# A macaron block in one kernel: hand-written orders for the opening and for the last four bodies

## What is computed

```python
x = L0_attn_x                                   # (2, 4096, 512)
x = x + 0.5 * _L0_ffn_ref(_layernorm(x), ...)   # first half
x = x + _L0_attn_ref(_layernorm(x), ...)        # causal linear attention, 16 heads of 32
x = x + 0.5 * _L0_ffn_ref(_layernorm(x), ...)   # second half

# at the end of _L0_ffn_ref
y = t + outs
yn = (y - mu) * jax.lax.rsqrt(var + 1e-05) * ln_g + ln_b

# attention, per head: phi(u) = elu(u) + 1
S = S + pk_t[..., :, None] * v_t[..., None, :]  # running state over the 4096 positions
z = z + pk_t
num = jnp.einsum('bhd,bhde->bhe', pq_t, S)
den = jnp.sum(pq_t * z, axis=-1, keepdims=True) + EPS
out = (num / den) @ Wo.T + bo
```

## Time and profile before

| | us |
|---|---|
| Time before, median of 3 runs | 940.27 (939.8 to 940.8) |
| Time of the profiled execution | 940.58 |
| Span of the profiled execution, first to last instruction | 938.8 |
| PE matmul busy | 898.5 (96%) |
| DVE busy | 827.4 (88%) |
| ACT busy | 758.4 (81%) |
| POOL busy | 711.6 (76%) |

### The profile page before, as it was taken

The page is one execution under the profiler, slowest core; times in us unless marked ns, Lnnn a source line. Parts: engine busy times, 40 slices in busy tenths (PEclk is TensorE's granted clock), DMA queues, the critical chain, the costliest instruction groups (busy, mean ns, idle before and its releaser), DMA issues. The chain is left out here.

```text
span 938.8 us, 29969 instructions
## 1 busy us (share of the span) xinstructions
PE 898.5 (96%) x10252; PEld 525.8 (56%) x10252; DVE 827.4 (88%) x1531; ACT 758.4 (81%) x1327; POOL 711.6 (76%) x875
## 2 busy tenths in 40 slices
PE   3899999999999999999999999999999999999974
PEld 2455556555555655555565555556565555655542
DVE  6888899999999999999999999999999999998764
ACT  5978788888888888888888888888888888888861
POOL 2277787788777788878778987777898777779761
PEclk9999999999999999999999999999999999999986
DMA  8286887866687666768767666876766787776762
GB/s 290 41 174 123 171 159 156 138 153 151 144 179 156 149 142 148 151 148 179 156 146 144 146 151 151 179 156 141 146 149 148 154 171 161 144 121 128 128 118 68
DMA packets 421405, 139.81 MB, mean 149 GB/s; under 512 B 402544, under 2 KB 402544, under 8 KB 421360
## 3 DMA queue, kind: packets, MB, share of 16 engines
q1 hardware_dynamic: 404496, 106.73, 60.5%
q10 hardware_dynamic: 16864, 32.51, 10.6%
HBM read 21.76 MB, written 16.78 MB: 41 GB/s over the span
## 5 line engine op out<-in xcount | busy, mean ns | idle before, releaser
L1302 PE MATMUL PJ<-wT,XT 128*128 128x512 f16 x2304 | 525.1, 379 | 1.7 <-DMA XT<-XH 1.4
L1302 PEld LDWEIGHTS PJ<-wT,XT 128*128 128x128 f16 x2304 | 216.6, 98 | 245.3 <-DMA XT<-XH 3.2
L459 POOL TENSOR_TENSOR A<-AM,A 128x512 f16<-128x512 f32 x256 | 292.5, 1162 | 35.4 <-ACT A L677 35.4
L1401 PE MATMUL PJ<-wT,AT 128*128 128x512 f16 x768 | 178.6, 383 | 1.2 <-DMA AT<-ATTN 1.2
L451 POOL TENSOR_SCALAR_AFFINE_SELECT AM<-AM 128x512 f32<-128x512 f32 x128 | 82.0, 641 | 113.1 <-ACT AM L667 113.1
L677 ACT ACTIVATE A<-AM 128x512 f16<-128x512 f32 x256 | 154.0, 630 | 12.6 <-POOL AM L451 11.3
L1372 PE MATMUL AV<-SS,QS 128*128 128x33 f16 x1024 | 112.3, 178 | 4.9 <-POOL A L459 4.4
L1375 PE MATMUL AV<-VN,A 128*128 128x33 f16 x3072 | 116.9, 178 | 0.0
L1401 PEld LDWEIGHTS PJ<-wT,AT 128*128 128x128 f16 x768 | 71.6, 98 | 79.8 <-issue 2.7
L1375 PEld LDWEIGHTS AV<-VN,A 128*128 128x128 f16 x3072 | 109.3, 96 | 3.7
L992 DVE TENSOR_TENSOR AM<-SC,causal 128x512 f32<-128x512 f32 x128 | 87.5, 684 | 22.9 <-PE SC L1352 22.9
(11 more groups left out here) (101 smaller groups left out, 1531.8 us busy)
## 6 DMA issues: line engine op xcount, KB each, us to landing
out_dram<-Y ACTq DMA_DIRECT2D x32, 512.0 KB, 3.1
X<-in_L_attn_x_dram ACTq DMA_DIRECT2D x30, 512.0 KB, 3.5
X<-in_L_attn_x_dram SPq DMA_DIRECT2D x2, 512.0 KB, 8.0
A<-in_L_attn_Wk_dram SPq DMA_DIRECT2D x1, 1024.0 KB, 8.3
A<-in_L_attn_Wq_dram SPq DMA_DIRECT2D x1, 1024.0 KB, 10.5
QS<-in_L_attn_Wv_dram SPq DMA_DIRECT2D x1, 1024.0 KB, 12.7
QS<-in_L_attn_Wo_dram SPq DMA_DIRECT2D x1, 1024.0 KB, 16.0
XT<-XH SPq DMA_TRANSPOSE x64, 3.4
```

The lines of the kernel that those rows point to most:

```text
L459: g.tensor_tensor(A[:, b, LO, hg], AM[:, k % 4], A[:, b, HI, hg], ALU.subtract).then_inc(a_lo.sem, 1)
L1302: ins = t_.matmul(PJ[b], XT[:, w, c, b * C:(b + 1) * C], wT[m_][:, m, c, :], start=(c, w, m) == todo[0], stop=(c, w, m) == todo[-1])
L1401: ins = t_.matmul(PJ[b], AT[:, b, w, c * C:(c + 1) * C], wT[3][:, m, c, :], start=(c, w, m) == todo[0], stop=(c, w, m) == todo[-1])
```

## The change

The bodies of steps 30 to 33 are taken out of `run` and written as one list per engine, `closing()`, with operations of steps 29 (`fourth`), 30 (`third`), 31 (`second`) and 32 (`last`). In step 31, the last with attention, all eight quads are masked on DVE (no `copy_scores`, no `cut`), and the low parts of the odd quads are computed on DVE (`split_a` of DVE, new, counted by `a_lo_last`) and those of the even quads on POOL. The last chunk's `rstd2`, `back_scale` and store go batch by batch (`rstd2_of_tile`, `store_tile`), so that two stores of 256 KB take the place of one. In all lists `opening()` is reordered; its operations are the same.

```diff
-            for s in range(steps - 4, steps + 2):
+            for s in range(steps - 4, steps - 2):
                 body(Step(0, s))
...
# SP opening, then its closing
                 early.turn_x(0)
                 early.turn_x(1)
+                first.turn_k(0)
+                first.turn_k(1)
                 first.turn_q(0)
-                first.turn_k(0)
                 first.turn_x(0)
+                first.turn_x(1)
                 first.turn_q(1)
-                first.turn_x(1)
-                first.turn_k(1)
                 second.turn_k(0)
...
+                fourth.turn_q(0)
+                fourth.turn_attn(0)
+                fourth.turn_attn(1)
+                fourth.turn_x(0)
+                fourth.turn_x(1)
+                fourth.turn_q(1)
+                fourth.turn_k(1)
+                third.turn_k(0)
+                third.turn_q(0)
+                third.turn_k(1)
+                third.turn_q(1)
+                third.turn_attn(0)
+                third.turn_attn(1)
+                second.turn_attn(0)
+                second.turn_attn(1)
...
-            sp.wait_ge(y_stored.sem, y_stored.at(steps - 1))
+            sp.wait_ge(y_stored.sem, y_stored.at(steps - 1, 1))
...
# POOL
+                    def rstd2_of_tile(b):
...
+                        g.tensor_scalar(var2[:, b:b + 1], stat2[:, b, 1:2], 1.0 + EPS, EPS * EPS, ALU.mult, ALU.add).then_inc(var2_done.sem, 1)
+                        pool.wait_ge(*var2_done.upto(back, b))
+                        g.tensor_tensor(rstd2[:, b:b + 1], var2[:, b:b + 1], neg_half[:, b:b + 1], ALU.pow).then_inc(rstd2_done.sem, 1)
...
                     def cut(b, hg):
-                        if not ATTEND:
+                        if not (ATTEND and PROJECT):
                             return
...
                     def split_a(b, hg):
...
+                        if not PROJECT and hg % 2:
+                            return
...
+                third.split_a(1, 3)
+                second.split_a(0, 0)
+                second.split_a(0, 2)
+                third.split_s(0)
+                third.split_s(1)
+                third.x1_bias()
+                second.rstd2_of_x2()
+                second.split_a(1, 0)
+                second.split_a(1, 2)
+                last.rstd2_of_tile(0)
+                last.rstd2_of_tile(1)
...
# ACT: its closing in part
+                third.sums(1)
+                third.attn_half(1)
+                second.split_a(0, 1)
+                second.split_a(0, 2)
+                third.v_half(1)
+                second.split_a(0, 3)
+                second.split_a(1, 0)
+                second.split_a(1, 1)
+                third.s_half(1)
+                second.sums(0)
+                second.back_scale(0)
+                second.split_a(1, 2)
+                second.split_a(1, 3)
+                second.back_scale(1)
+                second.attn_half(0)
+                second.sums(1)
+                second.attn_half(1)
+                second.store_y()
+                last.back_scale(0)
+                last.back_scale(1)
+                last.store_tile(0)
+                last.store_tile(1)
...
+                    def store_tile(b):
+                        act.wait_ge(*y_done.upto(back, b))
+                        a.dma_start(out[b, bass.ds(back * C, C), :], Y[:, b]).then_inc(y_stored.sem, 16)
...
# DVE
+                    def split_a(b, hg):
+                        if not ATTEND or PROJECT or hg % 2 == 0:
+                            return
+                        k = b * GROUPS + hg
+                        dve.wait_ge(*a_hi.upto(s, k))
+                        v.tensor_tensor(A[:, b, LO, hg], AM[:, k % 4], A[:, b, HI, hg], ALU.subtract).then_inc(a_lo_last.sem, 1)
...
# DVE opening, from the last weight on
-                first.phi_q(1)
+                first.low_q(1)
+                second.front_mean(0)
+                w_low(3, 0)
                 first.x_low(0)
                 second.front_stats(1)
-                w_low(3, 0)
-                second.front_mean(0)
-                first.low_q(1)
+                w_low(3, 1)
+                second.front_mean(1)
+                w_low(3, 2)
                 first.x_low(1)
+                w_low(3, 3)
                 first.low_v(0)
-                second.front_mean(1)
-                w_low(3, 1)
-                w_low(3, 2)
-                w_low(3, 3)
-                first.low_k(1)
+                first.low_v(1)
                 second.mask(0, 0)
...
# DVE closing, from the last step's first mask on
+                third.low_q(1)
+                third.add_s(0)
+                second.mask(0, 0)
+                second.mask(0, 1)
+                second.mask(0, 2)
+                third.attn_low(0)
+                third.low_v(0)
+                third.reciprocals(1)
+                third.quotient(1)
+                second.mask(0, 3)
+                third.attn_low(1)
+                second.split_a(0, 1)
+                third.low_v(1)
+                third.add_s(1)
+                second.mask(1, 0)
+                second.mask(1, 1)
+                second.split_a(0, 3)
+                second.split_a(1, 1)
+                third.add_out(0)
+                third.out_stats(0)
+                third.add_out(1)
+                third.out_stats(1)
+                third.out_mean(0)
+                third.out_mean(1)
+                second.mask(1, 2)
+                second.mask(1, 3)
+                second.reciprocals(0)
+                second.back_gain(0)
+                second.back_y(0)
+                second.quotient(0)
+                second.split_a(1, 3)
+                second.back_gain(1)
+                second.attn_low(0)
+                second.back_y(1)
+                second.reciprocals(1)
+                second.quotient(1)
+                second.attn_low(1)
+                second.add_out(0)
+                second.out_stats(0)
+                second.out_mean(0)
+                second.add_out(1)
+                second.out_stats(1)
+                second.out_mean(1)
+                last.back_gain(0)
+                last.back_y(0)
+                last.back_gain(1)
+                last.back_y(1)
...
# PE closing, from the projection of the last chunk on
+                third.project_k(0)
+                third.project_k(1)
+                third.project_q(0)
+                third.scores(1, 0)
+                third.project_q(1)
+                third.scores(1, 1)
+                third.scores(1, 2)
+                third.attend(0, 0)
+                third.attend(0, 1)
+                third.scores(1, 3)
+                third.project_v(0)
+                third.update(0, 0)
+                third.update(0, 1)
+                second.scores(0, 0)
+                second.scores(0, 1)
+                second.scores(0, 2)
+                third.attend(1, 0)
+                third.attend(1, 1)
+                second.scores(0, 3)
+                third.project_v(1)
+                second.scores(1, 0)
+                second.scores(1, 1)
+                third.update(1, 0)
+                third.update(1, 1)
+                third.project_out(0)
+                third.project_out(1)
+                second.scores(1, 2)
+                second.scores(1, 3)
+                second.attend(0, 0)
+                second.attend(0, 1)
+                second.attend(1, 0)
+                second.attend(1, 1)
+                second.project_out(0)
+                second.project_out(1)
```

More of the change, by code:

```diff
@@ L535, in _, with closing @@
             run(pool, body)
+            def closing():
+                fourth, third, second, last = ops(Step(0, steps - 3)), ops(Step(0, steps - 2)), ops(Step(0, steps - 1)), ops(Step(0, steps))
+                fourth.cut(1, 3)
+                fourth.spread_q(0)
+                fourth.split_a(1, 1)
+                fourth.split_a(1, 2)
+                fourth.split_a(1, 3)
+                fourth.rstd1_of_x1()
+                fourth.spread_k(1)
+                third.cut(0, 1)
+                third.split_a(0, 0)
+                fourth.spread_q(1)
+                third.cut(0, 3)
+                fourth.split_s(0)
+                fourth.split_s(1)
+                third.rstd2_of_x2()
+                third.split_a(0, 1)
+                third.split_a(0, 2)
+                third.split_a(0, 3)
+                third.spread_k(0)
+                third.spread_k(1)
+                third.spread_q(0)
+                third.cut(1, 1)
+                third.split_a(1, 0)
+                third.split_a(1, 1)
+                third.cut(1, 3)
+                third.spread_q(1)
+                third.split_a(1, 2)
+                third.split_a(1, 3)
[9 more added lines that the diff above has]
+                last.rstd2_of_tile(1)
+            closing()
         @block.scalar
@@ L1245, in opening @@
-                first.low_k(1)
+                first.low_v(1)
                 second.mask(0, 0)
```

(75 more changed lines are left out.)

232 lines of the change are left out of this document (161 added, 71 removed).

## The result

The changed kernel takes 934.0 us (median of 6 runs, 932.5 to 937.36), the kernel before 940.79 (6 runs beside it, 939.8 to 943.88): a ratio of 0.9929 [0.9905, 0.9954], which is 6.7 us less. The forecast was 932.8, 7.5 us less than the median known then. The profiled execution is the longest of the six: 937.36, with a span of 935.5, so the trace shows 3.3 us of gain where the ratio has 6.7.

The account below looks back on a forecast made before the run. The middle was taken as bound by TensorE, with gains only at the ends: 938.8 - 4.9 (tail) - 2.6 (opening) = 931.3 span; with 1.8 for execution and 0.3 for the profiled run's excess over the median, 932.8 us; range 927.8 to 937.4.

Parts of the forecast that it names:

- steps 1 to 3: Tail up to the end of the last two projections, reordered: that end moves from 928.03 to 926.0.
- Step 1: Tail: scores moved ahead of step 30's output projection, one new wait of 1.1 us; projection ends about 907.1, tile 0 attended 909.1.
- Step 2: Tail: attend(1,0) waits for quotient(0) behind nine VectorE operations until 912.7; TensorE idle 3.6 us, clock falls again.
- step 4: Final chain after TensorE's end: 5.0 us instead of 7.3 by splitting norm and store; store gains 0.6; end 933.9.
- The low parts: Four low parts moved to VectorE: 0.7 us each, 2.6 on VectorE, 4.6 off GpSimd; only the last on the path.
- Rival D: Low parts on VectorE and GpSimd exclude each other: two full exclusions of 1.16 us on the path, 935.1; chance 0.13.
- The opening: Start of the kernel, same operations in another order: 2.6 us gained, at most the 9.6 us of idle time.
- the second projection then follows at once, 0.7 earlier than before: Opening: first projection starts about 25.0 instead of 24.27, the second follows without a wait, 0.7 us earlier.
- SyncE's swap: Opening: turn_x(1) issued before turn_q(1), so project_k(1) starts at 53.0 instead of 55.80; 2.8 us, counted as 2.6.
- rival E: Loop: engines enter with another offset, a transpose late in each body; 0.5 us per body gives 947.3; chance 0.05.
- Rival B: Tail: the clock holds, first of the last projections takes 2.76 instead of 5.14 us; 930.4; chance 0.20.
- C: Opening gives nothing, VectorE's order only moves waits as it is busy 83% there; 935.4; chance 0.15.

Follow-up runs that it names:

- close_only: The new closing alone, with the old opening lists, against the kernel before: 938.07 us, ratio 0.9966.
- open_only: The kernel before with the five new opening lists alone: 937.67 us, ratio 0.9961 to the kernel before.
- exit_early: Changed kernel with the hardware loop one turn shorter and two more bodies written out behind it: 936.54 us, ratio 0.994 to the kernel before.
- tail_freed: Changed kernel with the last step's quotient put into X1 and one step 30 output projection between the two tiles' attends: 928.54 us, 0.9861 to the kernel before.
- y_at_once: Changed kernel with one rstd2 for both batches and one 512 KB store at the end: 937.13 us, ratio 0.9951 to the kernel before.
- new_again: The changed kernel unchanged, run again for a second profile: 934.5 us, ratio 0.9923 to the kernel before.
- sp_q_first: Changed kernel with turn_q(1) ahead of turn_x(1) again in SyncE's opening list: 933.61 us, ratio 0.9921 to the kernel before.
- freed_store_early: `tail_freed` with the loop-exit store of y moved four ScalarE operations up: 928.39 us, ratio 0.9868 to the kernel before.
- freed_store_held: `tail_freed` with the later loop-exit store of `store_held`: 929.6 us, ratio 0.9863 to the kernel before.
- store_held: Changed kernel with ScalarE's store of y at the loop's exit issued later: 934.43 us, ratio 0.9914 to the kernel before.

## Why the prediction was right, and where it was off

The direction held, and so did the size (6.7 of 7.5 us) and that both ends bring a gain. That the sum came so close is in part luck: the closing brought 3.0 us by `close_only` instead of 4.9, the opening 3.4 by `open_only` instead of 2.6, and the two errors have opposite signs. What failed is the reordering of the tail, steps 1 to 3. Step by step:

**The tail.** Forecast and trace, with 0.49 us taken off the trace since its last k projection starts at 878.28 instead of 877.79:

| | forecast | measured |
|---|---|---|
| step 30's output projections end | 907.15 | 908.97 |
| tile 0 attended | 909.1 | 911.04 |
| tile 1's attend starts | 912.7 | 915.32 |
| last two projections start | 918.0 | 920.31 |
| they end | 926.0 | 927.35 |
| last y ends | 931.0 | 932.50 |
| end | 933.9 | 935.0 |

Step 1 was too short by 1.8 us. Its one new wait was priced at 1.1; there were two in that place, 0.44 + 0.56, and a third of 1.37 before `scores(1,0)` at 902.86, 2.37 us together. `project`, split and turn of the last q are earlier in the lists, but the scores moved up still further. The two q transposes were issued at 890.68 and 896.03 and landed after 4.7 and 6.7 us, at 895.4 and 902.7, each just before the scores that need it. The waits make 1.3 of the 1.8 us; the other 0.5 isn't traced to an operation.

Step 2 named the right wait and the right operation behind it, but left a term out of the sum for VectorE: it put `rstd2` on GpSimd at 909.0 to 909.9 and took VectorE's own list as the limit, without ScalarE's scale (0.69 us), which stands between `rstd2` and `back_gain(0)`. From the last mean to `back_gain(0)` the trace has 1.99 us; two masks and a reciprocal fill all but 0.62 of it. So TensorE was idle for 4.28 us instead of 3.6, and without those 0.62 us it would be 3.66. `exit_early` shows that GpSimd's `x1_bias` isn't the cause: there it ended at 911.21, 0.41 us before the last mean, and `back_gain(0)` waited 0.63 all the same. `tail_freed` has neither this chain nor the 4.28 us, and 6 us less.

The clock fell as walked. Two things gave time back: the two projections took 7.04 us instead of 8.0, since the clock rose within them (0.93 in 924 to 926), and store to end 2.5 instead of 2.9. The chain of the last y took 5.15 against 5.0. From TensorE's end to the program's the trace gained 10.77 - 7.66 = 3.1 us, forecast 2.9; `y_at_once` measures 2.1 to 2.6 of it by the ratios and 2.5 by the traces, for the split of norm and store alone. So step 4 carries all or nearly all of the closing's gain (3.0). The reordering in steps 1 to 3, which was to bring 2.0 (928.03 to 926.0), brought 0.7 in this trace; over all eight profiles with this tail or nearly the same the stretch took 49.1 to 50.9 us, against 50.2 before, so no gain of the reordering is shown.

**The low parts** cost what the prediction said: 0.68 to 0.69 us each, none of 1.0. Rival D did not occur in this kernel: GpSimd stood idle at three of the four, as walked, and at the fourth the two overlapped by 0.21 us and GpSimd took 1.23 us instead of 1.16. In `tail_freed` the exclusion can be seen, on both sides:

```profile
901.93 0.68 DVE L1161 TENSOR_TENSOR A<-AM,A 128x512 f16<-128x512 f32 x1
...
902.15 1.47 POOL L490 TENSOR_TENSOR A<-AM,A 128x512 f16<-128x512 f32 x1 [1.79 <-ACT A L757]
...
903.59 1.19 POOL L513 TENSOR_TENSOR SS<-S,SC_HI 128x528 f16<-128x528 f32 x1
...
904.14 1.19 DVE L1161 TENSOR_TENSOR A<-AM,A 128x512 f16<-128x512 f32 x1
...
904.74 1.60 POOL L490 TENSOR_TENSOR A<-AM,A 128x512 f16<-128x512 f32 x1
```

Each time it is the one that began second that takes longer. GpSimd's low part at 902.15 overlaps VectorE's by 0.46 us and takes 0.31 more than 1.16. VectorE's at 904.14 overlaps GpSimd's `split_s` by 0.64 and takes 0.51 more than 0.68. GpSimd's at 904.74 overlaps that one by 0.59 and takes 0.44 more. The Trainium skill, "SBUF — State Buffer", "Who interferes with whom", has the two exclude each other; the trace agrees with that at the price of the overlap (less about 0.14 us), paid by the one that came second, and not with the 1.16 us each that rival D was priced at.

**The opening** was forecast at 2.6 us and brought 3.4 by the medians. By three marks of the trace (first projection, scores, second q projection of the first chunk), before 24.27, 50.87, 63.52 and after 25.20, 48.09, 59.85: 0.9 was lost ahead of the first, forecast 0.7. That agreement is luck: 0.74 of it is the landing of the first weight (TensorE's first matmul at 11.44 instead of 10.70), and the new order itself costs 0.2. The first stretch shrank from 26.60 to 22.89 us, by 3.7, forecast 2.3 (24.27 to 50.87 against 25.0 to 49.3); the second from 12.65 to 11.76, by 0.9, forecast 1.0. The step that failed is "the second projection then follows at once, 0.7 earlier than before": it starts at 28.98, 1.5 earlier, 3.8 us behind the first instead of 6.2, and the weight pieces behind it move with it. A third of that difference, 0.74 us, is the first projection itself (3.40 instead of 4.14 us), which the prediction left as it was. It isn't a lasting gain: in `new_again` the first projection took 4.46 us, the second began 4.8 behind it, and the first stretch was 23.94 us, 2.7 shorter than before and near the forecast 2.3. Calling SyncE's swap the largest step was too much as well: the trace of `sp_q_first` gives it 1.4 us of the second stretch, and its median none. Which of the five lists brings the rest wasn't measured, but for VectorE's, which alone loses.

**The middle** was costed at nothing by its 400 full us; the loop's exit was not looked at. The profiled execution lost 4.2 us between the opening's last mark and 878 (814.27 to 818.43), 0.64 + 2.22 - 0.41 = 2.45 of it in waits and 7.04 - 5.34 = 1.7 by the clock; this is rival E in small, a new offset that makes a transpose late, once and not in each body. Rival B did not come (clock 0.51 in 914 to 916), nor did C.

**Open.** Why the executions of one kernel lie so far apart: 5.5 us in 16 runs of the kernel before, 4.9 in the changed one, 5.3 in `freed_store_early`, 4.3 in `freed_store_held`, but 0.9 in `tail_freed` and 1.3 in `store_held`, all these with four to six runs. The landing of the first weight may be a part: TensorE's first matmul starts between 10.01 and 12.21 us in the profiles, at 11.44 in the changed kernel's slowest execution and at 10.30 in the 934.56 us of `new_again`. A late transpose at the loop's exit with its clock fall, 0.9 to 3.9 us, is of that size, but `store_held` has no such wait in its profile and the same median. Nor was it tried which of `tail_freed`'s two edits brings its 6 us.

## What to carry to other kernels

When a wait is put in place of another, follow the releaser through every engine up to its first instruction, with each engine's time in the sum: the walk had GpSimd's part of a chain over three engines and left out ScalarE's, 0.69 us. Then ask whether the operation has to wait for that chain at all: a tail in which the quotient no longer does, with one projection moved behind it, gained nearly as much again as the whole change. Splitting the last result's norm and store by the tiles as they finish was worth about 2.5 of the 6.7 us. A place ahead in a list doesn't make an operation the cause: compare its end with the other inputs of what follows. Hand-ordered lists that wait for one another are changed together: VectorE's new opening without the others' cost 9 us where all together gained 3.4.

## What the runs showed of the hardware

- A store of 512 KB issued within 0.5 us of two transposes (SBUF to SBUF) and the transposes hinder each other: 4.8 to 6.6 us from issue to landing for the transposes, 3.8 to 4.5 for the store. With 1.25 us or more between them it was 3.0 to 5.3 and 3.1 to 3.5.
- Whether the clock falls after some 2.5 us of idle TensorE isn't sharp: 2.22 us (loop's exit) and 2.58 (`tail_freed`) were followed by 7.04 us for two projections. 2.51 us was followed by 8.24 us for two in `freed_store_held` and by 2.76 for one, at a granted clock of 1.00, in `freed_store_early`, with the same instructions around it.
- VectorE's subtract of two SBUF tiles and GpSimd's subtract of the same kind take longer where they overlap, and only the one that began second: by 0.31, 0.44 and 0.51 us at overlaps of 0.46, 0.59 and 0.64 (`tail_freed`).
